# Attention gather: PSUM split as three places for sums and two for scores, and the score spreads placed inside the first half of a batch's sums

## The reference

```python
h = jnp.einsum('ni,hio->nho', x, W)                   # 8 heads of 64
s_src = jnp.einsum('nho,ho->nh', h, a_src)
s_tgt = jnp.einsum('nho,ho->nh', h, a_tgt)
e = s_src[src] + s_tgt[tgt]
e = jnp.where(e >= 0, e, NEG_SLOPE * e)
m = jax.ops.segment_max(e, tgt, num_segments=n)
ex = jnp.exp(e - m[tgt])
denom = jax.ops.segment_sum(ex, tgt, num_segments=n)
alpha = ex / (denom[tgt] + 1e-16)
msgs = h[src] * alpha[:, :, None]
out = jax.ops.segment_sum(msgs, tgt, num_segments=n)
```

## Time and profile before

| | us |
|---|---|
| median of three runs | 2799.72 |
| lowest and highest | 2782.97, 2802.28 |
| profiled execution, its own time | 2787.2 |
| its span in the trace | 2784.6 |
| TensorE busy in it | 2220.8 (80%) |
| VectorE busy | 1516.5 (54%) |
| GpSimd busy | 860.9 (31%) |
| mean granted TensorE clock | 0.926 of full |

### The profile page before, as it was taken

How to read it: one execution, slowest core, us unless ns; L and a number is a source line. 1 busy time by engine, 2 the same in 40 slices (tenths; PEclk the granted TensorE clock), 3 DMA queues, 4 the chain that set the end, 5 groups by cost and what they waited for, 6 DMA issues and landing times. The chain is left out here.

```text
span 2784.6 us, 33249 instructions
## 1 busy us (share of the span) xinstructions
PE 2220.8 (80%) x9870; PEld 1390.5 (50%) x9870; DVE 1516.5 (54%) x3018; ACT 688.8 (25%) x1786; POOL 860.9 (31%) x880
## 2 busy tenths in 40 slices
PE   0199996787888886489949768888888776999997
PEld 0056553333433344466626445656565664565664
DVE  6976665666676765333335547777777762111111
ACT  0011111111111112123312244444444123223232
POOL 2000002655656561035530066666666000000000
PEclk9999998999999998589979879999999885999999
DMA  1111112322322244523331167777777221000001
GB/s 44 36 61 75 60 60 81 87 79 80 86 77 84 75 82 65 179 42 57 58 89 43 45 197 200 199 199 198 196 197 186 43 64 29 0 0 0 0 0 37
DMA packets 112639, 236.09 MB, mean 85 GB/s; under 512 B 22424, under 2 KB 66859, under 8 KB 109800
## 3 DMA queue, kind: packets, MB, share of 16 engines
q0 software_dynamic: 56784, 160.68, 23.1%
q1 hardware_dynamic: 55704, 73.57, 7.9%
HBM read 193.62 MB, written 40.57 MB: 84 GB/s over the span
## 5 line engine op out<-in xcount | busy, mean ns | idle before, releaser
L608 POOL DMA_INDIRECT rows<-h_table,row_rel x372 | 358.5, 964 | 678.1 <-SPq L531 440.8
L2187 PE MATMUL p_ag<-rows_g,oh_g 128*128 128x260 f32 x1488 | 405.0, 412 | 108.3 <-DVE acc L2083 49.1
L2055 POOL DMA_INDIRECT rows_g<-g_table,row_src x372 | 351.8, 946 | 357.4 <-POOLq L95 144.2
L2187 PEld LDWEIGHTS p_ag<-rows_g,oh_g 128*128 128x128 f32 x1488 | 260.4, 194 | 183.3 <-issue 90.8
L860 PE MATMUL p_agg<-rows,oh 128*128 128x256 f32 x744 | 205.3, 412 | 35.6 <-DVE x L659 18.7
L2478 DVE SCALAR_TENSOR_TENSOR x<-p_yf,cw,x 128x256 f32<-128x256 f32 (+1 forms) x160 | 66.4, 478 | 306.4 <-PE p_yf L2569 306.4
L2100 DVE TENSOR_TENSOR rows_g<-rows_g,p_n 128x2048 f32<-128x2048 f32 x93 | 211.6, 2275 | 0.6 <-issue 0.6
L728 DVE TENSOR_TENSOR fT<-a_sb,p_sel 128x512 f32<-128x512 f32 x200 | 129.4, 684 | 114.4 <-PE p_sel L908 60.6
L860 PEld LDWEIGHTS p_agg<-rows,oh 128*128 128x128 f32 x744 | 137.5, 198 | 104.1 <-issue 55.2
L2083 DVE TENSOR_TENSOR acc<-acc,p_ag 128x520 f32 x186 | 128.7, 692 | 59.1 <-remote 33.9
L2569 PE MATMUL p_yf<-f,h_f 128*128 128x256 f32 (+1 forms) x640 | 145.3, 380 | 0.8 <-ACT h_f L2510 0.8
(11 more groups left out here) (433 smaller groups left out, 3474.9 us busy)
## 6 DMA issues: line engine op xcount, KB each, us to landing
h_table<-h_out SPq DMA_DIRECT2D x20, 1024.0 KB
where_g<-d_table SPq DMA_DIRECT2D x93, 128.0 KB
w<-in_L_ffn_W SPq DMA_DIRECT2D x16, 512.0 KB, 9.6
rows<-h_table,row_rel POOLq DMA_INDIRECT x372
rows_g<-g_table,row_src POOLq DMA_INDIRECT x372
g_table<-row SPq DMA_DIRECT2D x20, 260.0 KB
f<-in_L_ffn_W SPq DMA_DIRECT2D x16, 256.0 KB
x_acc<-x SPq DMA_DIRECT2D x1, 2560.0 KB
```

Of the source, the lines that this page charges most:

```text
L608: pool.indirect_dma_start(rows[:, r, j], None, st.h_rows, bass.IndirectOffsetOnAxis(ap=st.row_rel[:, at:at + 1], axis=0)).then_inc(gathere ...
L2055: pool.indirect_dma_start(rows[:, r, j], None, st.g_table, bass.IndirectOffsetOnAxis(ap=st.row_src[:, at:at + 1], axis=0)).then_inc(gather ...
L2187: last = pe.matmul(p_a[:, k % 2, h, 0:HALF], oh[:, r, j], rows[:, r, j, h * HALF:(h + 1) * HALF], start=j % SUP == 0, stop=j % SUP == SUP - 1)
```

## The change

The eight banks are split anew: two for p_n and three pairs for the sums (NS = 3). So a sum waits for the add of the sum three back, and the spread for batch s + 2 can be written only when batch s no longer needs its place. TensorE now spreads two batches ahead, all 12 matmuls inside the first two slots of sums: six before the first slot, six before the second. The filler is written into the unused columns of the sums' own bank; it has 252 columns instead of 384, stands in every batch from the third on, and waits for the place to be free. On VectorE, ohT is made for s + 3 at the head of a round instead of for s + 4 behind the scores, and the reads of tile_of stand right behind the weighing, before the adds.

```diff
+    NS = 3
...
-        p_n = ps("p_n", [P, NR, 512])
-        p_a = ps("p_ag", [P, 2, 2, 512])
+        p_n = ps("p_n", [P, 2, 512])
+        p_a = ps("p_ag", [P, NS, 2, 512])
...
-            tiles = None
             for s in range(NBATCH):
+                if 0 < s <= NBATCH - NR:
+                    turned_hot(s + NR - 1)
                 if s + 1 < NBATCH:
                     scores(s + 1)
-                if s + NR < NBATCH:
-                    turned_hot(s + NR)
                 weigh(s)
                 if s:
-                    for g in range(GR):
-                        add_sum(GR * (s - 1) + g, tiles[g])
-                tiles = tiles_of(s)
-            for g in range(GR):
-                add_sum(GR * (NBATCH - 1) + g, tiles[g])
+                    for g, tile in enumerate(tiles_of(s - 1)):
+                        add_sum(GR * (s - 1) + g, tile)
+            for g, tile in enumerate(tiles_of(NBATCH - 1)):
+                add_sum(GR * (NBATCH - 1) + g, tile)
...
-            for s in range(3):
+            for s in range(2):
                 for j in range(BATCH):
                     spread(s, j)
             for s in range(NBATCH):
                 r = s % RING
-                if 0 < s < NBATCH - 3:
-                    pe.matmul(p_n[:, (s + 3) % NR, P:], st.ident[:, :], st.iota[:, :].unsqueeze(1).broadcast_to([P, 3, P]),
-                              start=True, stop=True, skip_group_check=True)
+                k = GR * s
+                if s > 1:
+                    pe.wait_ge(agg_added, k - NS + 1)
+                    pe.matmul(p_a[:, k % NS, 0, HALF:], st.ident[:, :], st.qT[:, 0:512 - HALF], start=True, stop=True,
+                              skip_group_check=True)
                 pe.wait_ge(oh_ready, s + 1)
                 pe.wait_ge(msg_ready, s + 1)
                 for j in range(BATCH):
                     k = GR * s + j // SUP
-                    if j % SUP == 0 and k >= 2:
-                        pe.wait_ge(agg_added, k - 1)
+                    if s + 2 < NBATCH and j < 2:
+                        spread(s + 2, 2 * j)
+                        spread(s + 2, 2 * j + 1)
+                    if j % SUP == 0 and k >= NS:
+                        pe.wait_ge(agg_added, k - NS + 1)
                     for h in range(2):
-                        last = pe.matmul(p_a[:, k % 2, h, 0:HALF], oh[:, r, j], rows[:, r, j, h * HALF:(h + 1) * HALF],
+                        last = pe.matmul(p_a[:, k % NS, h, 0:HALF], oh[:, r, j], rows[:, r, j, h * HALF:(h + 1) * HALF],
                                          start=j % SUP == 0, stop=j % SUP == SUP - 1)
                     if j % SUP == SUP - 1:
                         last.then_inc(agg_done, 1)
-                    if s + 3 < NBATCH:
-                        spread(s + 3, j)
```

## The result

The changed kernel takes 2845.35 us (median of 4 runs, 2841.02 to 2847.6), the kernel before 2797.01 us (4 runs, 2782.97 to 2802.28): ratio 1.0187, 95% interval 1.0158 to 1.0216. It is slower, by 48 us. Its profiled execution took 2847.6 us with a span of 2844.7.

A forecast was written before the change was run, and what follows sets the result against it. The prediction took TensorE signals held while GpSimd issues gathers to bound the attention gather. The costlier spread distance gave +46 us, other parts and the start 0: 2799.7 + 46 = 2846 us, range 2755 to 2890.

The forecast's parts named there:

- the step that was called costly: Attention gather: spreads two batches ahead instead of three, inside the sums' first half, cost +23 to +69 us, taken as +46.
- Nobody is full, a wait sets the pace: Attention gather before the change: VectorE needs 5.3 us, TensorE and GpSimd about 5.0 each, yet a batch takes 6.07.
- Signals are held while GpSimd issues gathers: Attention gather: most TensorE signals are held during gathers and pass once GpSimd has been idle 1.2 to 1.9 us.
- The warning at the prediction's end: Attention gather: all would be upset if TensorE's signals were held by something else that the trace does not name.
- Each held n_ready makes a round of 6.2 and then 7.5 us: Attention gather: held rounds average 6.85 us, or 6.33 if one in four slips through; +0.26 to +0.78 us a batch.
- Size: Whole kernel: +46 us, all from the attention gather; its start counted as 0, with -7 us kept for the range.
- Third place worth nothing alone: TensorE's sums: start 0.7 to 0.8 us sooner after each weighing, of worth only where VectorE next waits for the sums.
- Reads of tile_of hidden, worth nothing on the path: VectorE: 0.68 us of reads go under the weighing, need falls from 5.3 to 4.6 us, but on an engine that waits.
- The clock: Rival, TensorE in the attention gather: idle lowers its clock, ten slow batches add 38 us, 2884 us; chance 0.06.
- What would show it: Attention-gather trace: L2093 idle over 100 us, L2084 hardly waiting, TensorE waiting for the weigh, L2101 alternating about 6 and 7.5 us.
- Where the faster rival was to decide: Attention gather: the rival of a faster kernel decides once n_ready is held in fewer than one batch in three.
- The faster rival: Attention gather: signals are held by TensorE standing at the removed wait, so -81 us, 2719 us, half a cure 2760; chance 0.16.

The follow-up runs named there:

- e2_near: Kernel before with only the spreads moved to two batches ahead, inside the first half of the sums; 2853.80 us, ratio 1.0296 to before.
- e5: Kernel before with three of four gathers left out from the seventh batch on (results not the reference's); 2715.74 us, ratio 0.9796 to before.
- e4: Changed kernel with three of four gathers left out from the seventh batch on (results not the reference's); 2638.06 us, ratio 0.9528 to before.
- e10: Changed kernel with all gathers, but weighing one of four rows and summing two of four (results not the reference's); 2752.74 us, ratio 0.9935 to before.
- e6: Changed kernel with spreads two ahead issued before TensorE's wait for weighted rows, the weigh's exponentials kept in SBUF; 2799.83 us, ratio 1.0101 to before.
- e8: Changed kernel with spreads ahead of TensorE's wait for weighted rows, and GpSimd allowed five batches ahead instead of six; 2798.82 us, ratio 1.0112 to before.
- e11: Changed kernel with a 128x1200 memset on GpSimd behind each batch's four gathers; 2762.07 us, ratio 0.9963 to before.
- e3: Changed kernel with each group of sums waiting for the add of two groups before, leaving the third place unused; 2838.86 us, ratio 1.0255 to before.
- e1: Kernel before with only VectorE's new order: tile_of reads behind the weigh, ohT ahead of the scores; 2790.44 us, ratio 1.0055 to before.
- e7: Changed kernel with its 252-column filler matmul given three times per batch; 2782.47 us, ratio 1.0040 to before.
- e12: Changed kernel with a 400-column memset on GpSimd behind each batch's four gathers, on another chip; 2635.86 us, ratio 1.0012 to before there.

## Why the prediction was right, and where it was not

The sign and most of the size (2846 predicted, 2845.35 measured) follow from the step that was called costly, and e2_near confirms that step alone. That the two times agree to 1 us is luck, as the points show. One by one:

- **Nobody is full, a wait sets the pace:** right. e5 brings the same engines to 5.33 us, where the prediction had 5.3 for VectorE and 5.0 for TensorE. TensorE's busy time there is 5.04 us, as predicted; its remaining 0.29 us is idle, 0.25 of it the wait for the add, which its sum left out.
- **Signals are held while GpSimd issues gathers:** that they are late behind rows of gathers is borne out by e4, e5 and e10, and the held n_ready pass 1.6 to 1.9 us after a row, within the 1.2 to 1.9 of the prediction. As a rule it is too simple: in e6, e8 and e11 most updates of agg_done pass at once while gathers are being issued, and one chip has no holding. What holds a signal stays open. The warning at the prediction's end, that something else might be behind it, was in place.
- **Each held n_ready makes a round of 6.2 and then 7.5 us:** the mean was right (+0.71 us against the ends of +0.26 and +0.78), the shape of the round was not, and this is the step that failed. The working let one n_ready in four slip through and gave each held one a round of 6.2 or 7.5 us, with GpSimd released once per round, for four gathers. Measured, 52 of 79 were at most 1 us late, and the held ones cost far more. In the trace it goes on from one batch to the next at once in each fourth round or so, and the row of eight gathers, 10 us, is what holds n_ready. Nineteen slots cost 4.41 us each over 6.07 and the other sixty gain 0.46 each, 83.8 - 27.6 = 56 us over 79 batches. That the sum of this is near the one predicted is luck.
- **Size:** 51.3 us between first and last weigh, against +46; the medians differ by 48.3. Of the 60.4 us between the two profiled executions, 7.7 lie ahead of the stage and 2.5 between its first gather and first weigh, which the prediction had at 0.
- **Third place worth nothing alone:** probably somewhat too low, since e3 gives 0.7% with an uncertainty of 0.5%. What the prediction did not see is that the edits taken together shorten TensorE's row by 0.64 us (e4 and e5). It counted this as slack that nobody needs, and with held signals nobody does.
- **Reads of tile_of hidden, worth nothing on the path:** the idle of 0.68 us is gone; e1 shows a loss of 0.55% for the new order, not zero.
- **The clock:** given a chance of 6% as a rival, it fell, 0.99 to 0.87, behind the standstills of 5 us. The 2.5 us in the earlier trace rows was no guide to these. The loss through it is within the measured 0.71: the sum matmuls took 418.8 us of TensorE's time instead of 405.0, and how much of these 13.8 us lay on the path stays open with e7.
- **What would show it:** L2093's "remote" idle over 100 us, L2084 less than before at the sums, and TensorE waiting for the weigh are in the rows above. The alternation of 6 and 7.5 us is not.
- **Where the faster rival was to decide:** n_ready held in fewer than one batch in three. It was over 1 us late in 27 of 79, just above that, and for a long slot in only 19 of 79, and still the kernel was slower, since each long slot cost 4.4 us. How often a signal is held was no good measure without how long.
- **The faster rival**, and the Trainium skill's rule that an attached update fires when its instruction completes ("PSUM — Partial Sum Buffer", section "Engine vs sequencer instructions"): the updates 5.7, 4.8 and 3.2 us late above speak against it on these chips. In e12's run, on the other chip, the trace agrees, with 0.01 us.

## What to carry to other kernels

How far ahead a signal is raised is a reserve against late signals: shorten it only after finding how late the worst one is, not the median, here 6.3 us in mid stage, behind a row of eight gathers that lasts 10, where the median of n_ready is 0.75. When a gathering engine waits for consumers in batches, look for rows of two batches back to back; breaking them with a pause of a microsecond took more off (ratio 1.0187 to 0.9963) than any other edit that kept all the work. And compare ratios on one chip, since a change can lose 2% on one and might gain on another.

## What was not expected of the hardware

- The kernel before took 2797.01, 2774.55, 2772.10, 2772.31 and 2632.72 us in the groups of runs. The last, 5% below, is from the chip on which TensorE's signals were not late.
- With a memset of 1.12 us between rows of gathers the median delay of TensorE's signals was 0.02 us, against 0.74 (n_ready) and 0.80 us (agg_done) over the stage without, though as many gathers were issued and GpSimd waited for nothing.
- In e6, with GpSimd issuing gathers in one row through the stage, 142 of 158 updates of agg_done came within 0.1 us of their matmul's end.
- A gather took 2 to 3 us instead of 0.95, one in four, once GpSimd ran ahead without waiting (e6 and e8), at 190 and 187 GB/s; e12 moved 212 GB/s without such gathers.
- 12 float32 matmuls of one column took 2.9 us of TensorE's time per batch, and its clock was 0.68 though the profile has the engine busy for the whole stretch.
